# A mixture-of-experts kernel on one core: the last expert prepares nothing for a next one, output tiles are copied and scattered tile by tile, and GpSimd waits once for VectorE

## The chip, the core and the metric

The kernel runs on one core of one Trainium2 chip. The metric is device microseconds (us) of one execution. Before the change it takes 1136.28 us, the median of 3 runs that lie between 1135.86 and 1139.66 us.

## The reference, cut to what matters

```python
# x (4, 512, 512), fside (4, 512, 512), cond (4, 128)
x = x + gated_recurrence(bi_wkv(x, fside, fside, w1, u1, cond))   # W_in, W_decay, W_gate, W_out: 512 x 512
x = x + moe(bi_wkv(x, fside, fside, w2, u2, cond))

def bi_wkv(r, k, v, w, u, cond):        # along t, per channel
    ek, ekv = exp(min(k, 30)), exp(min(k, 30)) * v
    # forward and backward sums a = a * decay + ekv, b = b * decay + ek
    num = fwd(ekv) + bwd(ekv) - ekv + exp(u + k) * v
    den = fwd(ek) + bwd(ek) - ek + exp(u + k)
    return sigmoid(r) * num / max(den, 1e-8) * (0.8 + 0.2 * tf)

def moe(xr):                            # 2048 tokens, 8 experts, top 2, 640 slots for each expert
    probs = softmax(xr @ Wg); gate, expert = top_k(probs, 2)
    h = relu(einsum("ecd,edf->ecf", dispatched, w1))     # w1 (8, 512, 2048)
    out = einsum("ecf,efd->ecd", h, w2)                  # w2 (8, 2048, 512)
    # each token's row is the gate-weighted sum of its two experts' rows
```

## The kernel before, in words

The program has two phases, and in both each engine runs an order of steps that is written out by hand; semaphores tie the engines together.

**The first phase** (`conditioning_and_routing`) works on 4 batches b of 512 tokens, with channels on the partitions. The sums of bi_wkv are made in 16 units u, each a pair of channel tiles of one batch and one of the two bi_wkv calls. For a unit, VectorE runs `backward` and `fold` (scans, L1149 to L1159), `complete` (L1166, L1169) and `ratio` (L1181); ScalarE makes exponentials (`own`, L778 and L782) and the reciprocal of the denominator through Ln and Exp (`first_reciprocal`, L796 and L798); GpSimd makes products of two SBUF tensors: `ek_products` (L356, L357), `products` (L363, L364) and `newton` (L376, L379), adds one term by an accumulating DMA (`own_add`, L370), and sends finished rows to their slots in DRAM (`dispatch`, L389). Two more steps of VectorE matter here. `first_out(b)` (L1194) multiplies `ratios` by the sigmoid `sig`, both in SBUF, and increments `s_r1`. `residual(b)` (L1216) reads the projection in PSUM and writes `xT`; TensorE's `gate(b + 1, k)` (L513) waits for it. `own(u)` on ScalarE waits for `newton(u - 2)`.

The orders that meet around the change are these. GpSimd: `dispatch(0, ...)`, `products(9)`, `ek_products(3, 0)`, `newton(8)`, `own_add(9)`, `products(10)`, `newton(9)`. VectorE: `backward(9)`, `first_out(2)`, `fold(9)`, `complete(9)`, `residual(1)`, `ratio(8)`, `backward(10)`.

**The second phase** (`experts`) runs 8 experts e one after the other. An expert has 640 slots in 5 tiles of 128 (`ST`), and `counts` tells how many hold tokens. The 2048 hidden columns are done in 16 steps of 128. TensorE's `up` makes a hidden step (L1566 to L1568, three products of split float32 parts), ScalarE applies Relu and rounds (L1684, `hh`), VectorE makes the remainder (L1750, `hl`), and TensorE's `down` adds the step into `ps_y` (L1586 to L1588), one PSUM bank for each slot tile, in the order of tiles 2, 3, 4, 0, 1; tiles 2 to 4 are left out where the count does not reach them. ScalarE and VectorE split the next weights in `split` (L1659, L1662; L1711, L1714). An expert with over 512 tokens is "wide": its hidden step is made in two halves.

Every expert also prepares the next one. SyncE loads its rows (`next_rows`), TensorE transposes one tile of them at a time (`turn`, L1536, behind q = 2 to 6 of the 8 rounds q), ScalarE and VectorE copy these into `next_xh` and `next_xl` (L1653, L1705), and at the end copy the whole into `xh` and `xl` (L1688, L1756). The last expert does all this too, though no expert follows.

At the end of an expert ScalarE and VectorE wait until its last `down` is complete (`s_f`), copy the 5 tiles of `ps_y` into `y`, scaled by the gate (L1696: even tiles; L1765: odd tiles), and GpSimd adds each tile's rows to the output in DRAM by an indirect DMA (L1516), tiles 0 to 4 in order. VectorE copies the next gate (L1736) only when all tiles are copied, then reads the count and branches, and only then makes `hl` of the next expert. TensorE meanwhile runs the first two `up` of the next expert.

```python
            for i in range(2, ST):
                with pe.If(count > i * P):
                    slot_tile(i)
            slot_tile(0)
            slot_tile(1).then_inc(s_f, 1)
```

## Time and profile before

| | us |
|---|---|
| median of 3 runs | 1136.28 |
| the profiled execution | 1134.53 |
| its span | 1132.8 |
| PE busy | 1037.4 (92%) |
| DVE busy | 652.9 (58%) |
| ACT busy | 525.7 (46%) |
| POOL busy | 280.2 (25%) |
| share of PE in the chain that ended last | 80% |

The span runs from the first to the last instruction of the program; 1.7 us of the execution lie around it. PE is TensorE's matmul row and PEld its weight loads, DVE is VectorE, ACT ScalarE, POOL GpSimd, SP SyncE; a "q" behind an engine's name is its sequencer. Matmuls are pipelined, so that their durations overlap; what a matmul costs is the distance to the next. "idle before" is the time in which the engine did nothing before an instruction, and the arrow names what released it. The first phase lasts until about 373 us, the experts until the end.

### The profile page before, as it was taken

The numbers are of one execution on the slowest core, as the hardware profiler recorded it, in microseconds if no ns is written. First come the engines' busy times: TensorE is split into PE (matmuls) and PEld (weight loads), VectorE is DVE, ScalarE is ACT, GpSimd is POOL, SyncE is SP. The second block draws the span as 40 slices with busy tenths as digits, with TensorE's granted clock in tenths as the row PEclk, the third lists the DMA queues.
The fourth block names the chain that finished last, engine by engine and source line by source line (L and its number), as shares of the span: only waits on it lengthen the run. The fifth ranks groups of instructions, "written<-read, shape, count | busy, mean of one in ns | idle before, by whom it ended". The sixth has DMA issues, their size and how long they took to land.

```text
span 1132.8 us, 17170 instructions
## 1 busy us (share of the span) xinstructions
PE 1037.4 (92%) x5054; PEld 817.2 (72%) x5055; DVE 652.9 (58%) x948; ACT 525.7 (46%) x844; POOL 280.2 (25%) x233
## 2 busy tenths in 40 slices
PE   3599995899997899999999999999999999999993
PEld 2334542355455799989998999898887888998883
DVE  5899999999983333343334333455564444334552
ACT  5776784676733233343334333445454334334442
POOL 4664746536755100030003000200203002000202
PEclk9999999898988899999999999999999999999997
DMA  6991431223325322262127222744536226222621
GB/s 213 327 303 19 112 78 72 38 93 95 130 47 190 140 74 74 74 166 74 74 74 167 74 74 74 170 145 167 167 111 210 74 74 160 100 91 92 169 74 22
DMA packets 67760, 132.67 MB, mean 117 GB/s; under 512 B 4982, under 2 KB 6042, under 8 KB 67736
## 3 DMA queue, kind: packets, MB, share of 16 engines
q1 hardware_dynamic: 54512, 106.58, 26.7%
q0 software_dynamic: 13008, 25.52, 11.7%
q8 instruction: 12, 0.20, 0.1%
q10 hardware_dynamic: 216, 0.28, 0.1%
q14 instruction: 12, 0.10, 0.0%
HBM read 91.99 MB, written 35.22 MB: 112 GB/s over the span
## 4 chain that ended last, share of the span: by engine, by line
PE 80%; DVE 6%; issue 5%; ACT 3%; DMA 3%; POOL 2%; DVEq 1%; ACTq 0%; SPq 0%; POOLq 0%
PE ps_mm L513 11%; PE ps_y L1586 10%; PE ps_y L1587 10%; PE ps_y L1588 10%; PE ps_h L1566 10%; PE ps_h L1567 10%; PE ps_h L1568 10%; PE ps_mm L530 2%; PE ps_t L1536 2%; PE ps_small L600 1%; DMA rows<-in_x_dram 1%; DVE sums_odd L1159 1%; POOL slots L389 1%; PE ps_x L530 1%; DMA f_rows<-in_fside_BxSxS_dram 1%
## 5 line engine op out<-in xcount | busy, mean ns | idle before, releaser
L1566 PE MATMUL ps_h<-xh,w1h 128*128 128x320 f32 (+4 forms) x768 | 244.8, 319 | 9.9 <-DVE hl L1750 4.4
L1567 PE MATMUL ps_h<-xl,w1h 128*128 128x320 f32 (+4 forms) x768 | 241.0, 314 | 0.0
L1568 PE MATMUL ps_h<-xh,w1l 128*128 128x320 f32 (+4 forms) x768 | 240.8, 313 | 0.0
L1516 POOL DMA_INDIRECT out_dram<-y,token x40 | 64.5, 1613 | 653.8 <-ACT y L1696 590.4
L1750 DVE SCALAR_TENSOR_TENSOR hl<-ps_h,hh 128x320 fp32r<-128x320 f32 (+1 forms) x192 | 106.8, 558 | 189.1 <-ACT hh L1684 183.0
L1586 PE MATMUL ps_y<-w2h,hh 128*128 128x512 f32 x528 | 206.9, 392 | 2.4 <-DVE hl L1750 2.4
L1587 PE MATMUL ps_y<-w2h,hl 128*128 128x512 f32 x528 | 206.3, 391 | 0.0
L1588 PE MATMUL ps_y<-w2l,hh 128*128 128x512 f32 x528 | 206.2, 390 | 0.0
L1714 DVE TENSOR_TENSOR w2l<-raw,w2h 128x512 fp32r<-128x512 f32 x128 | 88.5, 691 | 196.8 <-ACT w2h L1662 196.8
L1684 ACT ACTIVATE hh<-ps_h 128x320 fp32r<-128x320 f32 (+1 forms) x192 | 94.2, 491 | 225.4 <-PE ps_h L1568 225.4
L513 PE MATMUL ps_mm<-ratios,wm 128*128 128x512 f32 x372 | 168.3, 608 | 15.4 <-DVE xT L1216 13.2
L1662 ACT ACTIVATE w2h<-raw 128x512 fp32r x128 | 80.7, 631 | 211.9 <-PE ps_y L1588 211.9
L1566 PEld LDWEIGHTS ps_h<-xh,w1h 128*128 128x128 f32 x768 | 145.1, 189 | 18.1 <-issue 8.0
L1567 PEld LDWEIGHTS ps_h<-xl,w1h 128*128 128x128 f32 x768 | 145.2, 189 | 4.9
L1568 PEld LDWEIGHTS ps_h<-xh,w1l 128*128 128x128 f32 x768 | 145.1, 189 | 2.6
L513 PEld LDWEIGHTS ps_mm<-ratios,wm 128*128 128x128 f32 x372 | 71.2, 196 | 99.0 <-issue 95.4
L1588 PEld LDWEIGHTS ps_y<-w2l,hh 128*128 128x128 f32 x528 | 99.1, 188 | 21.6
L1586 PEld LDWEIGHTS ps_y<-w2h,hh 128*128 128x128 f32 x528 | 99.2, 188 | 20.6 <-issue 3.2
L1587 PEld LDWEIGHTS ps_y<-w2h,hl 128*128 128x128 f32 x528 | 99.2, 188 | 17.1
L1711 DVE TENSOR_TENSOR w1l<-raw,w1h 128x512 fp32r<-128x512 f32 x128 | 88.3, 689 | 16.2 <-ACT w1h L1659 12.1
L1659 ACT ACTIVATE w1h<-raw 128x512 fp32r x128 | 79.8, 623 | 0.0
L1159 DVE TENSOR_TENSOR_SCAN sums_odd<-ps_decay,sums_odd 128x511 f32<-128x511 f32 x32 | 38.3, 1256 | 3.5 <-ACT sums_odd L789 3.5
(206 smaller groups left out, 1179.3 us busy)
## 6 DMA issues: line engine op xcount, KB each, us to landing
raw<-in_L_ffn_w_dram SPq DMA_DIRECT2D x64, 1024.0 KB, 6.9
slots<-r_rows SPq DMA_DIRECT2D x8, 1302.5 KB, 20.2
rows<-slots SPq DMA_DIRECT2D x8, 1302.5 KB, 8.0
rows<-in_x_dram SPq DMA_DIRECT2D x4, 1024.0 KB, 5.3
sums_even<-eukv POOLq DMA_DIRECT2D x8, 512.0 KB, 5.2
sums_odd<-eukv POOLq DMA_DIRECT2D x8, 512.0 KB, 6.0
out_dram<-rows SPq DMA_DIRECT2D x4, 1024.0 KB, 4.7
f_rows<-in_fside_BxSxS_dram SPq DMA_DIRECT2D x3, 1024.0 KB, 5.4
```

Source lines behind the costliest of these rows:

```text
L513: last = nc.tensor.matmul(ps_mm[:, k % 3, :], wm[:, m, dt, e * P:(e + 1) * P], ratio_of(0, b)[:, dt], start=(dt == 0), stop=(dt == CT - 1))
L1566: nc.tensor.matmul(o, w1h[:, j, dt, :], xh[:, dt, lo:hi], start=(dt == 0), stop=False)
L1567: nc.tensor.matmul(o, w1h[:, j, dt, :], xl[:, dt, lo:hi], start=False, stop=False)
L1568: last = nc.tensor.matmul(o, w1l[:, j, dt, :], xh[:, dt, lo:hi], start=False, stop=(dt == CT - 1))
L1586: nc.tensor.matmul(ps_y[:, i, :], hh[:, j, tok], w2h[:, j], start=first, stop=False)
L1587: nc.tensor.matmul(ps_y[:, i, :], hl[:, j, tok], w2h[:, j], start=False, stop=False)
L1588: return nc.tensor.matmul(ps_y[:, i, :], hh[:, j, tok], w2l[:, j], start=False, stop=last)
L1662: a.activation(w2h[:, (j + 1) % 2], raw2[:, bass.ds((c + (j + 1) // FC) % 2, 1), (j + 1) % FC] .rearrange("p o n -> p (o n)"), ACT.Copy).t ...
L1684: a.activation(hh[:, j % 2, lo:hi], ps_h[:, bank, 0:hi - lo], ACT.Relu).then_inc(s_hh, 1 if wide else 2)
L1711: v.tensor_tensor(w1l[:, j % 2], raw1[:, bass.ds((c + j // 2) % 2, 1), :, (j + 2) % FC * P:((j + 2) % FC + 1) * P] .rearrange("p o t q -> ...
L1714: v.tensor_tensor(w2l[:, (j + 1) % 2], raw2[:, bass.ds((c + (j + 1) // FC) % 2, 1), (j + 1) % FC] .rearrange("p o n -> p (o n)"), w2h[:, ( ...
L1750: v.scalar_tensor_tensor(out=hl[:, j % 2, lo:hi], in0=ps_h[:, bank, 0:hi - lo], scalar=0.0, in1=hh[:, j % 2, lo:hi].bitcast(F32), op0=ALU.max,
```

## The change

There are three parts.

1. In the first phase GpSimd waits for `s_r1` to reach 3, which is the end of VectorE's `first_out(2)`, before `newton(8)`.
2. At an expert's end, ScalarE and VectorE no longer wait for the whole last `down`. TensorE increments a semaphore of its own for tiles 2, 3, 4 and 0 as each is finished (at once for a tile that is left out). ScalarE copies tiles 2, 4, 0, VectorE 3, 1, and GpSimd scatters in the order 2, 3, 4, 0, 1. An expert that is not wide still has its tile 4 neither computed nor copied.
3. The last expert loads no rows, turns nothing, copies nothing into `next_xh`, `next_xl`, `xh`, `xl` and the next gate and token, and leaves out the last `split`.

```diff
@@ gpsimd_program, first phase
         ek_products(3, 0)
+
+        pool.wait_ge(s_r1, 2 + 1)
         newton(8)
@@ experts
+    s_out = {i: sem(f"output_tile_{i}_done") for i in (2, 3, 4, 0)}
...
+    EVEN_ORDER, ODD_ORDER = (2, 4, 0), (3, 1)
+    Y_EVEN, Y_ODD = len(EVEN_ORDER), len(ODD_ORDER)
@@ sync_program
         def expert(e, last):
-            next_rows(e)
+            if not last:
+                next_rows(e)
@@ gpsimd_program, second phase
-            for i in range(ST):
+            for i in (*range(2, ST), 0, 1):
                 if i % 2 == 0:
-                    pool.wait_ge(s_ya, Y_EVEN * (e + 1) + i // 2 + 1)
+                    pool.wait_ge(s_ya, Y_EVEN * (e + 1) + EVEN_ORDER.index(i) + 1)
                 else:
-                    pool.wait_ge(s_yv, Y_ODD * (e + 1) + i // 2 + 1)
+                    pool.wait_ge(s_yv, Y_ODD * (e + 1) + ODD_ORDER.index(i) + 1)
@@ down
             for i in range(2, ST):
                 with pe.If(count > i * P):
-                    slot_tile(i)
-            slot_tile(0)
+                    done = slot_tile(i)
+                    if last:
+                        done.then_inc(s_out[i], 1)
+                if last:
+                    with pe.Else():
+                        pe.sem_inc(s_out[i], 1)
+            done = slot_tile(0)
+            if last:
+                done.then_inc(s_out[0], 1)
             slot_tile(1).then_inc(s_f, 1)
@@ tensor_program
                 with pe.Else():
-                    turn_one_of(e, q, 0, ST + 1)
+                    with pe.If(e < NE - 1):
+                        turn_one_of(e, q, 0, ST + 1)
@@ scalar_program (vector_program alike)
                         if j == FC - 1:
                             with act.If(c > NC - 2):
-                                act.wait_ge(s_xh, ST * (e + 2))
-                                a.activation(xh[:], next_xh[:], ACT.Copy).then_inc(s_cur_h, 1)
-                        split(e, c, j)
-                act.wait_ge(s_f, e * FT + (FT + 2))
+                                with act.If(e < NE - 1):
+                                    act.wait_ge(s_xh, ST * (e + 2))
+                                    a.activation(xh[:], next_xh[:], ACT.Copy).then_inc(s_cur_h, 1)
+                                    split(e, c, j)
+                            with act.Else():
+                                split(e, c, j)
+                        else:
+                            split(e, c, j)
...
-                for i in range(0, ST if wide else ST - 1, 2):
-
+                for i in EVEN_ORDER if wide else (2, 0):
+
+                    act.wait_ge(s_out[i], e + 1)
@@ vector_program
-                dve.wait_ge(s_f, e * FT + (FT + 2))
                 dve.wait_ge(s_y0, 1)
                 dve.wait_ge(s_token, e + 1)
-                for i in range(1, ST if wide else ST - 1, 2):
+                for i in ODD_ORDER:
+                    if i == 1:
+                        dve.wait_ge(s_f, e * FT + (FT + 2))
+                    else:
+                        dve.wait_ge(s_out[i], e + 1)
```

GpSimd's order around `newton(8)` before the change, from `products(9)` on (`recip_ready` is `s_rec`):

```order
L363 TENSOR_TENSOR eukv<-euk,kT 128x512 [waits euk_ready]
L364 TENSOR_TENSOR eukv<-euk,kT 128x512
L356 TENSOR_TENSOR ekv<-ek,kT 128x512 [waits ek_ready]
L357 TENSOR_TENSOR ekv<-ek,kT 128x512
L376 TENSOR_TENSOR sums_even<-sums_even,euk 128x512 [waits recip_ready]
L376 TENSOR_TENSOR sums_even<-sums_even,euk 128x512
L379 TENSOR_TENSOR sums_even<-sums_even,euk 128x512 [waits even_own_term_added]
L379 TENSOR_TENSOR sums_even<-sums_even,euk 128x512
```

and with the change:

```order
L363 TENSOR_TENSOR eukv<-euk,kT 128x512 [waits euk_ready]
L364 TENSOR_TENSOR eukv<-euk,kT 128x512
L356 TENSOR_TENSOR ekv<-ek,kT 128x512 [waits ek_ready]
L357 TENSOR_TENSOR ekv<-ek,kT 128x512
L376 TENSOR_TENSOR sums_even<-sums_even,euk 128x512 [waits recip_ready,r1_ready]
L376 TENSOR_TENSOR sums_even<-sums_even,euk 128x512
L379 TENSOR_TENSOR sums_even<-sums_even,euk 128x512 [waits even_own_term_added]
L379 TENSOR_TENSOR sums_even<-sums_even,euk 128x512
```

Nothing has moved; the first `newton` product has a second semaphore to wait for.

ScalarE's order at the end of an expert that is not wide, before, from the last step's `split` to the copies into `y` (`hidden_used` is `s_f`):

```order
L1659 ISA
L1659 ACTIVATE w1h<-raw 128x512
L1661 REGISTER_ALU
L1662 REGISTER_ALU [waits hidden_used]
L1662 ACTIVATE w2h<-raw 128x512
L1673 REGISTER_ALU
L1673 COMPARE_AND_BRANCH
L1690 ISA
L1691 REGISTER_ALU [waits hidden_used]
L1696 ACTIVATE y<-ps_y,gate 128x512 [waits token_ready,y_cleared,gate_ready]
L1696 ACTIVATE y<-ps_y,gate 128x512
```

and with the change (the line numbers are those of the changed file, L1676 and L1679 the split's, L1719 the copy's):

```order
L1705 UNCONDITIONAL_BRANCH
L1676 ISA
L1676 ACTIVATE w1h<-raw 128x512
L1678 REGISTER_ALU
L1679 REGISTER_ALU [waits hidden_used]
L1679 ACTIVATE w2h<-raw 128x512
L1709 UNCONDITIONAL_BRANCH
L1690 REGISTER_ALU
L1690 COMPARE_AND_BRANCH
L1713 REGISTER_ALU
L1719 ACTIVATE y<-ps_y,gate 128x512 [waits token_ready,y_cleared,output_tile_2_done,gate_ready]
L1719 ACTIVATE y<-ps_y,gate 128x512 [waits output_tile_0_done]
```

The wait for the whole `down` ahead of the copies is gone, and each copy waits for its tile. The split now stands in the program twice, once behind the copy of `xh` (ahead of this piece) and once, here, for the rounds that have no such copy.

GpSimd's scatters of the first expert, before:

```order
L1504 COPY token<-next_token 128x5 [waits next_token_ready]
L1508 COPY next_token<-rows 128x5 [waits token_ready,next_rows_in]
L1516 DMA out_dram<-y,token 2048x512 [waits y_cleared,y_even]
L1516 DMA out_dram<-y,token 2048x512 [waits y_odd]
L1516 DMA out_dram<-y,token 2048x512 [waits y_even]
L1516 DMA out_dram<-y,token 2048x512 [waits y_odd]
L1516 DMA out_dram<-y,token 2048x512 [waits y_even]
```

and with the change:

```order
L1511 COPY token<-next_token 128x5 [waits next_token_ready]
L1516 COPY next_token<-rows 128x5 [waits token_ready,next_rows_in]
L1524 DMA out_dram<-y,token 2048x512 [waits y_cleared,y_even]
L1524 DMA out_dram<-y,token 2048x512 [waits y_odd]
L1524 DMA out_dram<-y,token 2048x512 [waits y_even] x2
L1524 DMA out_dram<-y,token 2048x512 [waits y_odd]
```

These are tiles 2, 3, then 4 and 0 from ScalarE, then 1.

## Rows read from the trace of the kernel before

**Rows 1.** Timeline, TensorE: start us, us, instruction, [idle before <- releaser].

```profile
203.00 6.04 PE L513 MATMUL ps_mm<-ratios,wm 128*128 128x512 f32 x8 [13.18 <-DVE xT L1216]
```

**Rows 2.** Timeline, VectorE, 181 to 207 us.

```profile
181.57 11.10 DVE L1194 SCALAR_TENSOR_TENSOR ratios<-ratios,neg_scale,sig 128x2048 f32<-128x2048 f32 x1
...
192.59 4.79 DVE L1159 TENSOR_TENSOR_SCAN sums_odd<-ps_decay,sums_odd 128x511 f32<-128x511 f32 x4
...
198.53 3.67 DVE L1169 TENSOR_SCALAR sums_odd<-sums_odd,den_min 128x512 f32<-128x512 f32 x2
...
204.76 2.05 DVE L1181 SCALAR_TENSOR_TENSOR ratios<-sums_even 128x1024 f32<-128x1024 f32 x1
```

**Rows 3.** Timeline, GpSimd, 180 to 200 us.

```profile
180.70 1.28 POOL L363 TENSOR_TENSOR eukv<-euk,kT 128x512 f32<-128x512 f32 x1
...
184.38 1.26 POOL L357 TENSOR_TENSOR ekv<-ek,kT 128x512 f32<-128x512 f32 x1
185.60 2.47 POOL L376 TENSOR_TENSOR sums_even<-sums_even,euk 128x512 f32<-128x512 f32 x2
188.04 2.48 POOL L379 TENSOR_TENSOR sums_even<-sums_even,euk 128x512 f32<-128x512 f32 x2
...
198.51 1.79 POOL L363 TENSOR_TENSOR eukv<-euk,kT 128x512 f32<-128x512 f32 x1
```

**Rows 4.** Line L1194, all its instructions: duration ns min/median/max.

```profile
L1194 DVE SCALAR_TENSOR_TENSOR ratios<-ratios,neg_scale,sig x4: 1285/2344/11100, 58.9 to 263.8; 128x2048 f32<-128x2048 f32 x3, 128x1024 f32<-128x1024 f32 x1
```

**Rows 5.** Timeline, ScalarE, 188 to 204 us.

```profile
190.61 1.34 ACT L778 ACTIVATE euk<-kT,cap_u 128x512 f32<-128x512 f32 x2 [5.75 <-POOL sums_even L379]
```

**Rows 6.** Waits of VectorE, 205 to 320 us: us in total, times, longest.

```profile
DVE sums_odd L1159 <- ACT sums_odd L789: 1.8, 1, 1.8
DVE xT L1216 <- PE ps_mm L530: 1.1, 1, 1.1
```

**Rows 7.** Busy time by window: PE, PEld, DVE, ACT, POOL, PEclk, DMA share, GB/s.

```profile
203.00:208.00 5.00, 5.00 (x6) 2.16 (x7) 4.89 (x5) 4.94 (x6) 3.55 (x3) 0.52 0.01 3
```

**Rows 8.** Waits of TensorE, 400 to 1120 us.

```profile
PE ps_h L1566 <- DVE hl L1750: 2.6, 3, 0.9
PE ps_y L1586 <- DVE hl L1750: 2.4, 3, 1.2
PE ps_h L1566 <- DVE w1l L1711: 1.7, 2, 0.9
PE ps_h L1566 <- issue: 0.6, 3, 0.3
```

**Rows 9.** Timeline, VectorE, from the first expert to the second.

```profile
491.98 1.41 DVE L1765 TENSOR_SCALAR y<-ps_y,gate 128x512 f32<-128x512 f32 x2 [1.88 <-PE ps_y L1588]
494.10 0.17 DVE L1736 COPY gate<-next_gate 128x5 f32<-128x5 f32 x1 [0.71 <-ACT y L1696]
495.85 0.89 DVE L1750 SCALAR_TENSOR_TENSOR hl<-ps_h,hh 128x320 fp32r<-128x320 f32 x2 [1.58 <-issue]
```

**Rows 10.** The chain that ended last, last expert: start us, us, what.

```profile
1104.39 0.44 PE ps_t L1536 x4
```

**Rows 11.** Timeline, TensorE, the last `down`: end of tile 2, end of tile 1.

```profile
1112.77 0.39 PE L1588 MATMUL ps_y<-w2l,hh 128*128 128x512 f32 x1
...
1114.13 0.39 PE L1588 MATMUL ps_y<-w2l,hh 128*128 128x512 f32 x1
```

**Rows 12.** Timeline, GpSimd, the end: the first and the last of five scatters.

```profile
1116.23 1.57 POOL L1516 DMA_INDIRECT out_dram<-y,token  x1 [53.01 <-ACT y L1696]
...
1123.64 1.54 POOL L1516 DMA_INDIRECT out_dram<-y,token  x1 [0.30 <-issue]
```

**Rows 13.** DMA issues of 1116 to 1119 us (two scatters): us from issue to landing.

```profile
out_dram<-y,token POOLq DMA_INDIRECT x2, 4.9
```

**Rows 14.** DMA issues of 1124 to 1133 us (the last scatter).

```profile
out_dram<-y,token POOLq DMA_INDIRECT x1, 2.7
```

**Rows 15.** DMA queues, 490 to 1133 us: the instruction queue's packets, MB, share.

```profile
q14 instruction: 1, 0.01, 0.0%
```

More of the change, by code:

```diff
@@ L1497, in gpsimd_program, with expert @@
         g.memset(y[:], 0.0).then_inc(s_y0, 1)
-        def expert(e, first):
+        def expert(e, first, last=False):
             pool.wait_ge(s_next_token, e + 1)
@@ L1520, in gpsimd_program @@
         expert(0, True)
-        with pool.Fori(1, NE) as e:
+        with pool.Fori(1, NE - 1) as e:
             expert(e, False)
+        expert(NE - 1, False, True)
         pool.wait_ge(s_add, 16 * ST * NE)
@@ L1678, in body @@
                             with act.If(c > start - 1):
-                                token_high(e, tile_no(c * 2 + more))
+                                with act.If(e < NE - 1):
+                                    token_high(e, tile_no(c * 2 + more))
                         act.wait_ge(s_f, hidden + 1)
@@ L1693, in body @@
                 act.wait_ge(s_token, e + 1)
-                for i in range(0, ST if wide else ST - 1, 2):
+                for i in EVEN_ORDER if wide else (2, 0):
+                    act.wait_ge(s_out[i], e + 1)
                     a.activation(y[:, i], ps_y[:, i, :], ACT.Copy, scale=gate[:, i:i + 1]).then_inc(
-                        s_ya, 2 if i == ST - 3 and not wide else 1)
+                        s_ya, 2 if i == 2 and not wide else 1)
             by_width(act, e, body)
@@ L1745, in body @@
                             with dve.If(c > start - 1):
-                                token_low(e, tile_no(c * 2 + more))
+                                with dve.If(e < NE - 1):
+                                    token_low(e, tile_no(c * 2 + more))
                         for k in range(2 if wide else 1):
@@ L1754, in body @@
                             with dve.If(c > NC - 2):
[L1755 to L1761 removed]
+                                with dve.If(e < NE - 1):
+                                    dve.wait_ge(s_xl, ST * (e + 2))
+                                    v.tensor_copy(xl[:], next_xl[:]).then_inc(s_cur_l, 1)
+                                    dve.wait_ge(s_next, 16 * (e + 1))
+                                    dve.wait_ge(s_gate, e + 1)
+                                    v.tensor_copy(next_gate[:], rows[:, :, bass.ds(e + (C + 1), 1)].rearrange("p i o -> p (i o)")).then_inc(s_next_gate, 1)
+                                    split(e, c, j)
+                            with dve.Else():
+                                split(e, c, j)
+                        else:
+                            split(e, c, j)
                 dve.wait_ge(s_y0, 1)
                 dve.wait_ge(s_token, e + 1)
[L1764 removed]
+                for i in ODD_ORDER:
+                    if i == 1:
+                        dve.wait_ge(s_f, e * FT + (FT + 2))
+                    else:
+                        dve.wait_ge(s_out[i], e + 1)
                     v.tensor_scalar(y[:, i], ps_y[:, i, :], gate[:, i:i + 1], None, ALU.mult).then_inc(s_yv, 1)
```

17 lines of the change are left out of this document (6 added, 11 removed).

## The prediction

> **What bounds the kernel now.** I read the page's chain first. It lies on TensorE for 80% of the span (the table above), so a change pays where TensorE stands still, where it works for nothing, or behind its last matmul. There are three such places. In the first phase it stands still for 13.18 us until 203.00, until VectorE's `residual` writes `xT` [rows 1]. Between experts it waits 2.6 + 2.4 us for VectorE's `hl`, 1.7 us for `w1l`, and 0.6 us for nothing that shows, behind such a wait [rows 8]; inside an expert it never waits. At the end, five scatters follow its last matmul [rows 11, 12].
>
> **Part 1, GpSimd's wait.** VectorE's `first_out(2)` begins at 181.57 and takes 11.10 us [rows 2]; the same line usually takes 2.34 [rows 4]. GpSimd runs eight products of two SBUF tensors without a break from 180.70 to 188.04 + 2.48 = 190.52 [rows 3] (two of `products(9)`, two of `ek_products(3, 0)`, four of `newton(8)`). VectorE's instruction ends at 192.67, 2.15 us behind the last of them: it was held for the whole series, and then ran. With the wait, GpSimd stops behind `ek_products(3, 0)`, at 184.38 + 1.26 = 185.64 [rows 3]. VectorE then ends at 185.64 + 2.2 = 187.8, 4.8 us earlier. Its four scans take 4.7 more, to 192.5. `newton(8)` runs beside them, from 187.9 to 187.9 + 4.9 = 192.8 instead of 190.5, and I take scans as not held: the four of 192.59 take 4.79 [rows 2], 1.2 each, and one of their inputs lies in PSUM.
>
> The next step holds a second gain. `complete(9)`'s two clamps took 3.67 us [rows 2], because `products(10)` began at 198.51 [rows 3], just as they did. `products(10)` waits for ScalarE's `own(10)`, which waits for `newton(8)` [rows 5]. It now begins at 192.9 and needs 2.5 us (four instructions, two of which take 1.34 [rows 5]), so `products(10)` starts at 195.4. Now `complete(9)` lies ahead of it. Its first instruction takes what lies between the scans' end, 192.59 + 4.79 = 197.38, and the clamps at 198.53: 1.2 us. Its clamps took 3.67 while GpSimd's two products ran from 198.5 to 201.3, some 2.8; without those, 0.9 [rows 2, 3]. `complete(9)` waits for the term that GpSimd adds behind `newton(8)`, for which I put 0.2 as its issue. So it ends at 192.8 + 0.2 + 1.2 + 0.9 = 195.1 instead of 198.53 + 3.67 = 202.2. `residual(1)` starts some 7.0 us earlier, and so does TensorE, at 196.0 instead of 203.0.
>
> The Trainium skill ("SBUF — State Buffer", section "Who interferes with whom") says that a VectorE instruction with two SBUF inputs and a GpSimd instruction that reads SBUF exclude each other, and that the one that issues first keeps the shared pair for its whole instruction. Two SBUF inputs is what L1194 has and the scans (one input in PSUM) have not, so kind and place agree. But one instruction's length would end the hold at 181.98, and the row shows eight [rows 2, 3].
>
> Do the 7.0 us last? `newton(8)` is 2.3 us later, but ScalarE's next step behind `own(10)` needs `complete(9)`, so it runs at 195.4 instead of 202.2. VectorE's `ratio(8)` now meets `products(10)` and `newton(9)` at 197.8; it took 2.05 in a like place [rows 2], and if held throughout it would end near 203.9, 3 us before its old end of 206.8 and 4 short of the full shift. VectorE idles 1.8 and 1.1 us for others by 272 us [rows 6] and twice more for 0.7 and 0.5, which takes such a lag up. I see nothing else that is bound to a fixed time. **Term: -7.0**, between -3 (the lag is not taken up) and -9.2.
>
> The lower bound is TensorE's clock. In its first 5 us after the wait the granted clock is 0.52, that is 1.2 GHz [rows 7]; six matmuls end where at 2.4 GHz some 2.2 us would have been saved. After 6 us of idleness it may come back sooner. I take it as unchanged.
>
> **Part 2, tiles one by one, between experts.** VectorE copies the gate at 494.10, behind ScalarE's last `y` copy, and makes `hl` only at 495.85, 1.58 us of its sequencer (the count's load and a branch) behind [rows 9]. Both engines had stood idle until `down` was complete, VectorE 1.88 us, and it then makes two copies in 1.41 us from 491.98 on [rows 9], ScalarE three until 494.0. With the change tiles 2, 3 and 4 are copied under `down`, and only tile 0 (ScalarE, a tile ahead of the end) and tile 1 (VectorE) come near its end. VectorE's is then the last: 491.98 + 0.7 = 492.7 instead of 494.0. So gate and `hl` come 1.3 us earlier, more than any of the waits. I count the two lines that name `hl` and the 0.6 behind them, 5.6 us, less the 0.6 of an expert of under 384 tokens, where VectorE itself comes late from its own `w2l` and the copies gain nothing, less 0.5 for residues: **-4.5**, between -1 (if the 1.58 does not move with the copies) and -5.6. The 1.7 us for `w1l` stay: it waits behind ScalarE's copy of `xh`, which every expert but the last keeps. The tile semaphores are increments on matmuls that are there anyway. One more `If` around `turn` costs TensorE nothing, since its sequencer is ahead inside an expert: no wait there [rows 8].
>
> **Part 3, the last expert.** Five `turn`s go, 0.44 us each on the chain [rows 10]: **-2.2**. Steps without a turn already follow each other without an idle microsecond, so nothing else comes to bound them. The copies into `xh`, `xl` and the last split go too (2.35 us on ScalarE); they lay beside `down` and by themselves give 0, but without them both engines are free when tile 2 is done. The 1.3 MB of rows that are not loaded had no one waiting.
>
> **The end.** Tile 2's last matmul starts at 1112.77, tile 1's at 1114.13 [rows 11], so the first copy and the first scatter come 1.36 us earlier. The five scatters are spaced (1123.64 - 1116.23) / 4 = 1.85 us by GpSimd itself [rows 12], whatever tile they hold, and so the last is issued 1.36 earlier as well. But it is another tile. This expert has at most 320 tokens, so the last scatter was tile 4, without a row, and landed in 2.7 us [rows 14]; now it is tile 1, with 128 rows, and such scatters take 4.9 [rows 13]. The end moves by -1.36 + 4.9 - 2.7 = **+0.8**, between -1.4 (landing as before) and +1.5.
>
> **Sum.** -7.0 - 4.5 - 2.2 + 0.8 = -12.9. Against the profiled execution's 1134.5 this gives 1121.6; the median of the runs lies 1.75 above that execution, so 1136.3 - 12.9 = **1123.4 us**. Runs of this kernel tell a difference from none at about 0.3%, 3.4 us.
>
> **Rivals.**
> - *The hold moves.* `ratio(8)` or a later step is held by a longer series of products, and VectorE's lag reaches TensorE. For it: 11.10 us shows that a series can hold VectorE throughout [rows 2]. Against it: the slack [rows 6]. Part 1 gives -3: 1127.4. Chance 0.15.
> - *The boundary does not shrink.* VectorE's `hl` hangs on something other than the copies. For it: 1.58 us with no releaser [rows 9]. Part 2 gives -0.5: 1127.4. Chance 0.11.
> - *The clock comes back with the shorter wait.* Part 1 gives -9.2: 1121.2. Chance 0.12.
> - *L1194 was not held by GpSimd's series.* By instruction-long exclusion VectorE would have run from 181.98, the 11.10 us have another cause, and the wait gives 0: 1136.3 - 5.9 = 1130.4. This is what the rule of the section cited above would make of it. Against it: 2.15 us from the series' end to the instruction's. Chance 0.03 alone, and 0.03 together with the boundary that does not shrink (1136.3 - 0.5 - 2.2 + 0.8 = 1134.4, no change that can be told).
> - *Slower, by code that no longer stays resident.* ScalarE's and VectorE's loop bodies now hold the split twice, and the other rounds jump over the first copy. In 640 us of experts the instruction queue moves one packet [rows 15], so today all loops are resident. If the jump cost a reload on each of the 32 rounds, at 1.58 us (the longest unexplained gap [rows 9]) that reached TensorE in full, it would lose 32 x 1.58 = 51 us: 1174. It decides from 0.5 us a round, since 32 x 0.5 = 16 is 12.9 + 3.4. Against it: the code grows by about 20 instructions an engine. Chance 0.03.
>
> The Trainium skill ("Runtime: NRT & Kernel Launch", section "Instruction fetch mechanics") says that a taken branch out of a window of two blocks of 256 instructions stalls for a fetch. By that the bodies still fit and this rival falls; no row shows the window.
>
> **Numbers.** The forecast has 0.53, with its own range 1121 to 1126. The range of 8 in 10 takes in the clock and the two rivals at 1127.4 with a margin: 1120 to 1128.5. Faster: 0.53 + 0.15 + 0.11 + 0.12 + 0.03 = 0.94; same 0.03; slower 0.03.
>
> **What would show it.** Right: L1194 near 181.6 takes about 6.3 us and ends near 187.8; the two clamps behind take 0.9; TensorE restarts near 196 and the experts begin 7 us earlier; the waits for `hl` between 400 and 1110 us fall from 5.0 to about 1; the last expert has no L1536; the last scatter starts 8.15 us behind the last matmul's start and not 9.5, and needs about 4.9 to land. Wrong: L1194 still over 10 us, or another VectorE step in the first phase grown by several; TensorE restarting at 196 with the experts less than 5 us earlier; idle TensorE inside experts or packets of the instruction queue there; a last landing much over 5 us.

## The result, and the profile after

The changed kernel takes **1124.97 us**, the median of 6 runs (1121.84 to 1130.62); the kernel before took 1136.07 in 6 runs beside them. The ratio is 0.9891, 95% interval [0.9871, 0.9910]: 11.1 us less in the medians. The forecast was 1123.4, with a range of 1120.0 to 1128.5. In the experiments below the changed kernel was measured again (e4): 1125.34, ratio 0.9900 [0.9876, 0.9924].

Its first profiled execution was the longest of its six. So two executions stand here, that one ("first") and the one of e4 ("second"):

| us | before | after, first | after, second (e4) |
|---|---|---|---|
| the execution | 1134.53 | 1130.62 | 1125.55 |
| span | 1132.8 | 1128.8 | 1123.8 |
| TensorE restarts | 203.00 | 197.08 | 196.53 |
| first `up` of the experts | 374.83 | 373.93 | 369.68 |
| first `up` to the start of the last `down` matmul | 739.30 | 735.03 | 734.29 |
| idle TensorE from 392 us to there | 7.4 | 4.3 | 3.7 |
| from there to the end of the span | 18.67 | 19.87 | 19.79 |

Without the row of idle time, the last three rows are parts of the span and add up to it: in the second execution 5.15 + 5.01 - 1.12 = 9.0 us less than the profiled execution of before. The other 2 us lie in that execution of before: it was 1.5 to 3.1 us below the medians of its kernel (1136.07 to 1137.66 from one set of runs to the next). Below, "lead" is by how much earlier TensorE starts a matmul than in that one execution of before; at 262 us it is the matmul that starts there at 262.50, at 323 us the one at 323.20.

The timeline of TensorE, VectorE and GpSimd in the first execution answers to [rows 1 to 3]:

```profile
197.08 6.23 PE L515 MATMUL ps_mm<-ratios,wm 128*128 128x512 f32 x8 [3.96 <-DVE xT L1218]
...
181.82 7.45 DVE L1196 SCALAR_TENSOR_TENSOR ratios<-ratios,neg_scale,sig 128x2048 f32<-128x2048 f32 x1
189.19 4.79 DVE L1161 TENSOR_TENSOR_SCAN sums_odd<-ps_decay,sums_odd 128x511 f32<-128x511 f32 x4
193.90 1.46 DVE L1168 TENSOR_TENSOR sums_odd<-sums_odd,euk 128x1024 f32<-128x1024 f32 x1
195.40 0.88 DVE L1171 TENSOR_SCALAR sums_odd<-sums_odd,den_min 128x512 f32<-128x512 f32 x2
...
182.15 1.28 POOL L363 TENSOR_TENSOR eukv<-euk,kT 128x512 f32<-128x512 f32 x1
...
185.83 1.27 POOL L357 TENSOR_TENSOR ekv<-ek,kT 128x512 f32<-128x512 f32 x1
189.34 2.49 POOL L376 TENSOR_TENSOR sums_even<-sums_even,euk 128x512 f32<-128x512 f32 x2 [2.24 <-DVE ratios L1196]
191.79 2.49 POOL L379 TENSOR_TENSOR sums_even<-sums_even,euk 128x512 f32<-128x512 f32 x2
194.28 1.31 POOL L370 DMA_DIRECT2D sums_odd<-eukv  x1
```

`first_out(2)` (now L1196) ends at 189.27, 2.17 us behind the end of `ek_products(3, 0)` at 187.10: held for four products and not eight. The two clamps take 0.88 together and not 3.67, and TensorE's wait is 3.96 us long and not 13.18.

Executions differ by some microseconds in when VectorE comes to this instruction (179.58 to 183.32), so the cleanest measure counts from its start to TensorE's restart. That is 21.4 us in all four profiled executions without the wait, and with the wait in this place 14.1 or 15.3: 7.4 us less where GpSimd's first product had begun before VectorE's instruction, 6.2 where VectorE had begun first.

The waits of TensorE from 400 to 1120 us in the second execution answer to [rows 8]:

```profile
PE ps_h L1575 <- issue: 2.7, 4, 1.2
PE ps_y L1595 <- DVE hl L1774: 0.5, 1, 0.5
PE ps_h L1575 <- DVE hl L1774: 0.3, 1, 0.3
```

The waits for `hl` fell from 5.0 to 0.8 us. "issue" rose from 0.6 to 2.7: two of its four stand at the two boundaries where TensorE waited 1.7 us in all for `w1l` before, and are 1.06 and 1.21 us long.

### The profile page after: what moved, and what is told of

It is laid out like the page before. It is cut to its first block, busy times and chain, and to the rows that moved or that the text cites. A ratio compares the mean times of both kernels' runs of the same rounds, so it can differ in the third digit from the quotient of the medians.

```text
span 1128.8 us, 17219 instructions
## 1 busy us (share of the span) xinstructions
PE 1040.3 (92%) x5034; PEld 816.5 (72%) x5035; DVE 644.6 (57%) x939; ACT 519.7 (46%) x836; POOL 279.3 (25%) x232
## 4 chain that ended last, share of the span: by engine, by line
PE 64%; issue 1%; POOL 1%; DVEq 0%; DVE 0%; ACT 0%; POOLq 0%
PE ps_y L1595 11%; PE ps_y L1596 11%; PE ps_y L1597 11%; PE ps_h L1575 10%; PE ps_h L1576 10%; PE ps_h L1577 10%; PE ps_t L1545 1%; POOL out_dram L1524 1%; DVEq L1650 0%; DVE y L1797 0%; DVE hl L1774 0%; ACT y L1719 0%; DVE gate L1759 0%; DVEq L1773 0%; DVEq L1763 0%
## 5 line engine op out<-in xcount | busy, mean ns | idle before, releaser
L1679 ACT ACTIVATE w2h<-raw 128x512 fp32r x127 | 80.1, 631 | 210.2 <-PE ps_y L1597 210.2
L1676 ACT ACTIVATE w1h<-raw 128x512 fp32r x127 | 79.2, 623 | 0.0
```

Of the source, the lines that this page charges most:

```text
L1679: a.activation(w2h[:, (j + 1) % 2], raw2[:, bass.ds((c + (j + 1) // FC) % 2, 1), (j + 1) % FC] .rearrange("p o n -> p (o n)"), ACT.Copy).t ...
```

## The experiments

The kernel before was run beside each set of runs, and every ratio is to it. Each kernel was run 6 times (e2 and e3 12 times), e5 and e8 once.

| run | median us | ratio [95%] | first `up` | up to last `down` | end |
|---|---|---|---|---|---|
| e1 wait only | 1130.10 | 0.9943 [0.9923, 0.9963] | 370.22 | 740.23 | 18.68 |
| e2 tiles only | 1136.05 | 0.9995 [0.9978, 1.0013] | 372.51 | 736.40 | 20.82 |
| e3 last expert only | 1135.25 | 0.9984 [0.9970, 0.9999] | 376.87 | 737.04 | 18.74 |
| e4 changed, again | 1125.34 | 0.9900 [0.9876, 0.9924] | 369.68 | 734.29 | 19.79 |
| e5 tail order | 1117.79 (one) | | 364.69 | 733.98 | 17.33 |
| e6 tail skip | 1121.22 | 0.9859 [0.9831, 0.9887] | 368.31 | 735.76 | 15.78 |
| e7 wait earlier | 1127.45 | 0.9897 [0.9868, 0.9927] | 370.15 | 737.85 | 19.97 |
| e8 pause | 1130.41 (one) | | 374.16 | 734.40 | 19.67 |
| e9 scatters late | 1125.25 | 0.9899 [0.9871, 0.9928] | 369.78 | 733.22 | 20.05 |
| e10 products(15) later | 1125.20 | 0.9892 [0.9861, 0.9923] | 371.27 | 734.87 | 19.69 |
| e11 two waits | 1126.31 | 0.9915 [0.9886, 0.9944] | 370.12 | 734.48 | 19.70 |
| e12 combined | 1117.65 | 0.9832 [0.9808, 0.9855] | 365.85 | 734.38 | 15.76 |

The three last columns are of the profiled execution, as in the table above ("end" is from the start of the last `down` matmul on). A single one of them moves without a cause in the edit: e1, which changes nothing in the experts, has 0.9 us more there than before, and e2, which changes nothing ahead of them, begins them 2.3 us earlier. Over all, the experts begin at 372.5 to 376.9 us in the four executions without GpSimd's wait (mean 374.6) and at 364.7 to 373.9 in the ten with it (mean 369.4).

### e1: the wait alone

```diff
         ek_products(3, 0)
+        pool.wait_ge(s_r1, 2 + 1)
         newton(8)
```

> The kernel before with GpSimd's one wait alone. Theory A (forecast): VectorE's first_out(2) (L1194) ends near 188 to 189, TensorE restarts near 197 instead of 203.0, the experts' first up comes 6 to 7 us earlier (near 368) and the time is 6 to 7 us less, a ratio of 0.9940 to 0.9947. Theory B (read from the profile of the changed kernel, where TensorE led by 7.4 us at 262 us and by only 0.9 us at 374): the lead is given back between 290 and 374 us whatever the execution, because what follows there has its own pace (a clamp of VectorE held by GpSimd, the clock, the loads of rows): the experts start 0 to 2 us earlier and the time is 0 to 2 us less, 0.9980 to 1.0000. Theory C: the loss in that one execution was chance, half of the executions have it: 3 to 4 us less, 0.9965 to 0.9975.

The ratio 0.9943 is 6.5 us less (4.2 to 8.8 by its interval), which is theory A's amount. TensorE restarted at 196.01, 7.0 us earlier, and led by 8.0 us at 262. But the experts began at 370.22, only 4.6 us earlier, which lies between the theories. What was lost lies in VectorE's timeline near 291 us, here of e4, which is alike:

```profile
290.91 3.64 DVE L1171 TENSOR_SCALAR sums_even<-sums_even,den_min 128x512 f32<-128x512 f32 x2
...
291.75 1.28 POOL L363 TENSOR_TENSOR eukv<-euk,kT 128x512 f32<-128x512 f32 x1
292.98 1.28 POOL L364 TENSOR_TENSOR eukv<-euk,kT 128x512 f32<-128x512 f32 x1
```

and of e6, where it did not happen:

```profile
291.01 1.07 DVE L1171 TENSOR_SCALAR sums_even<-sums_even,den_min 128x512 f32<-128x512 f32 x2
...
294.07 1.30 POOL L363 TENSOR_TENSOR eukv<-euk,kT 128x512 f32<-128x512 f32 x1
295.29 1.29 POOL L364 TENSOR_TENSOR eukv<-euk,kT 128x512 f32<-128x512 f32 x1
```

`complete(14)`'s second clamp met `products(15)` and was held for its two products, 2.6 us. In e6 the four DMA instructions of the dispatch ahead of `products(15)` ended later, and it began behind the clamps. With the wait for `s_r1` and `products(15)` in its place, the hold is there in six profiled executions of eight; without that wait in one of four (e3, at 297.8). In the six, TensorE's lead fell by 3.4 us between 262 and 323 us; in e5 and e6 it rose by 0.2. TensorE's own waits put the price a little lower: from 300 to 322 us it waits 3.1 to 3.6 us in the six (1.3 for ScalarE's `z_gate`, the rest for VectorE's) and 1.0 in e5 and e6, so the hold costs it 2.1 to 2.6 us.

Whether the hold comes goes with TensorE's clock some 40 us earlier. Over 244 to 264 us the granted clock (the third number from the end of a row) is 0.91 in all seven of these executions with the hold and 0.83 in all five without it. Here are the windows of before, without the hold, and of e4, with it:

```profile
244.00:264.00 20.00, 18.92 (x84) 12.59 (x83) 18.99 (x37) 13.79 (x17) 6.06 (x5) 0.83 0.13 22
```

```profile
244.00:264.00 20.00, 19.31 (x82) 12.29 (x81) 19.30 (x34) 16.20 (x21) 10.16 (x9) 0.91 0.16 27
```

The two agree in twelve of twelve; that one makes the other was not tested. In e4 `newton(13)` ended 1.3 us earlier than in e6 (286.27 and 287.58) while the clamps began at nearly the same time (290.91 and 291.01), and this brings `products(15)` nearer to them.

### e2: tile by tile alone

```diff
-                act.wait_ge(s_f, e * FT + (FT + 2))
+                    act.wait_ge(s_out[i], e + 1)
...
+            for i in (*range(2, ST), 0, 1):
```

> The kernel before with the tile-by-tile copies and scatters alone; the last expert still prepares a next one. Forecast: TensorE's idle time between 392 us and the last down falls from 7.4 us by 4.5 us at the seven boundaries, the end (last scatter is the full tile 1, lands in 4.9 us and not 2.7) costs 0.8 more: 3.7 us less, ratio 0.9967. Rival: hl comes late for another reason than the copies (count load and branch), idle time stays near 7 us: 0 to +0.8 us, ratio 1.0000 to 1.0007.

The experts took 2.9 us less and TensorE's idle time fell by 3.5, but the end took 2.15 us more and not 0.8: 0.75 us less in the trace, and no difference that the runs could tell. ScalarE's and GpSimd's timeline at the end:

```profile
1105.58 2.35 ACT L1698 ACTIVATE xh<-next_xh 128x2560 fp32r<-128x2560 f32 x1
...
1108.86 1.26 ACT L1706 ACTIVATE y<-ps_y,gate 128x512 f32<-128x512 f32 x2
...
1110.38 1.57 POOL L1519 DMA_INDIRECT out_dram<-y,token  x1 [53.17 <-ACT y L1706]
...
1117.79 1.54 POOL L1519 DMA_INDIRECT out_dram<-y,token  x1 [0.30 <-issue]
```

With the last expert's copy of `xh` and the split still there, tile 2's copy starts at 1108.86, level with the last matmul's start (1108.91). In the changed kernel's first execution it starts 1.10 us before (1107.86 against 1108.96). So the last scatter starts 8.88 us behind that matmul and not 7.91. The end needs parts 2 and 3 together.

### e3: the last expert's omissions alone

```diff
-            next_rows(e)
+            if not last:
+                next_rows(e)
...
+                    with pe.If(e < NE - 1):
+                        turn_one_of(e, q, 0, ST + 1)
```

> The kernel before with the last expert's omissions alone (no rows loaded, nothing turned, copied or split for a next expert); the last expert's copies into y still wait for its whole down. Forecast: five turns of 0.44 us go from TensorE, 2.2 us less, ratio 0.9981, and nothing else moves: the last scatter starts as far behind the last matmul as before (9.5 us) and TensorE's idle time at the boundaries stays near 7.4 us. Rival: the jump over the second copy of the split in every round costs an instruction load or late commands, which would show as more idle TensorE inside the experts: 0 to 10 us more.

As forecast: up to the last `down` 2.26 us less, the end as before (18.74), the waits of TensorE between the experts the same to 0.1 us; the ratio 0.9984 is 1.8 us. That 2.26 meets the forecast 2.2 so closely is partly luck, since e1 shows 0.9 us of difference in the same stretch for nothing. No cost of the second split is to be seen.

### e4: the changed kernel again

> The changed kernel again, for a second profiled execution beside the first, whose 1130.6 us was the longest of six. Theory C: in another execution the lead of TensorE at 262 us (7 us) reaches the experts with at least 4 us left and the profiled time is near 1124. Theory B: the experts' first up is again near 374 and the lead is lost in the same place between 290 and 350 us. By either the median ratio is 0.987 to 0.991.

The lead was 7.9 us at 262 us, 4.5 at 323 and 5.15 at the experts' start. The hold at 291 us is there too, so the fall up to 323 us is not the first execution's own, as theory B has it. What made that execution so long comes later: its lead was 4.1 us at 323 us, but it reached the experts with 0.9. That part is theory C's. The waits of TensorE from 323 to 374 us, the first execution and then e4 (without those of about the same length in both):

```profile
PE ps_t L1621 <- DVE w2l L1400: 4.0, 1, 4.0
...
PE ps_mm L547 <- ACT rows L860: 2.8, 2, 1.4
...
PE ps_small L754 <- DVE dest L1282: 0.7, 1, 0.7
```

```profile
PE ps_t L1621 <- DVE w2l L1400: 3.1, 1, 3.1
...
PE ps_small L754 <- DVE dest L1282: 1.6, 1, 1.6
PE ps_mm L547 <- ACT rows L860: 0.3, 1, 0.3
```

From 323 us on the first execution falls 3.8 us behind e4. The waits for ScalarE's rows and for `w2l` are 3.4 us longer in it and the one for `dest` 0.9 shorter, 2.4 in all; why ScalarE and VectorE came late there was not followed further.

### e5 and e6: the last expert's scatters

e5 changes their order, e6 leaves out the empty ones:

```diff
-            for i in (*range(2, ST), 0, 1):
+            for i in (2, 0, 1, 3, 4) if last else (*range(2, ST), 0, 1):
```

```diff
+            if last:
+                count = pool.value_load(counts[0:1, NE - 1:NE], min_val=1, max_val=CAP)
...
+                if last and i > 1:
+                    with pool.If(count > i * P):
+                        scatter(i, s_part[i])
```

> The changed kernel, but the last expert's five scatters go in the order of tiles 2, 0, 1, 3, 4, so that the last one has no row. If the landing of the last scatter is what gave back most of the earlier start, the last scatter again starts about 7.9 us behind the last matmul's start (all copies are done 3 us before), lands in 2.7 us and not 5.2, and the end comes 17.3 us behind the last matmul's start and not 19.8. If the queue works tiles one after the other, so that the empty ones wait behind the full ones, it lands later than 2.7 us and the end gains less than 1 us.

> The changed kernel, but in the last expert GpSimd reads the count and leaves out the scatters of tiles that hold no token (3 and 4 here). Two scatters fewer at 1.85 us each: the last one starts 7.9 - 3.7 = 4.2 us behind the last matmul's start, lands in about 5.2, and the end is 3.7 us earlier than with all five, 16.1 us behind the last matmul. Against the kernel before: ratio 0.9870 to 0.9880 where the changed kernel has 0.9891 to 0.9900. Rival: the branches and waits on GpSimd, or the copy of tile 1, set the pace instead: less than 2 us.

The last scatter of e5, in GpSimd's timeline and in the DMA issues (us to landing at the end of the row):

```profile
1106.57 1.54 POOL L1524 DMA_INDIRECT out_dram<-y,token  x1 [0.31 <-issue]
```

```profile
out_dram<-y,token POOLq DMA_INDIRECT x1, 2.7
```

and of e6, whose last scatter is the third:

```profile
1108.28 1.54 POOL L1508 DMA_INDIRECT out_dram<-y,token  x1 [0.30 <-issue]
```

```profile
out_dram<-y,token POOLq DMA_INDIRECT x1, 5.3
```

Last `down` matmuls started at 1098.67 and 1104.07, so the last scatters start 7.90 and 4.21 us behind them, and the ends are 17.33 and 15.78: both as expected (17.3, 16.1). In the changed kernel GpSimd's sequencer leaves its wait for the last landing 5.25 us behind that scatter's start; before it was 2.74. The full tile at the end costs 2.5 us. (e5's single time also has the earliest first phase of all: its `first_out(2)` starts at 179.58, 2.0 us before that of the profiled execution of before, which its edit does not explain.)

### e7: the wait two products earlier

```diff
         products(9)
+        pool.wait_ge(s_r1, 2 + 1)
         ek_products(3, 0)
-        pool.wait_ge(s_r1, 2 + 1)
         newton(8)
```

> The changed kernel with GpSimd's wait two instructions earlier, ahead of ek_products(3, 0) instead of behind it, so that the series beside L1196 (first_out(2)) is two products and not four. If VectorE is held until the series ends, L1196 ends 2.2 us behind the end of products(9), near 185.8, and takes about 2.5 us less than with the wait in its place (4.0 to 4.9 against 6.2 to 7.4); its scans then end near 190.6. ek_products and newton(8) then run as one series of six from 186 to 193.5, and complete(9)'s clamps are held to its end, so TensorE restarts at 196 to 197, as in the changed kernel: ratio like the changed kernel's, 0.988 to 0.991. If VectorE were held for one instruction only and its length came from something else, L1196 would keep its 6 to 7 us.

VectorE's and GpSimd's timeline:

```profile
182.19 5.01 DVE L1195 SCALAR_TENSOR_TENSOR ratios<-ratios,neg_scale,sig 128x2048 f32<-128x2048 f32 x1
...
193.34 2.77 DVE L1170 TENSOR_SCALAR sums_odd<-sums_odd,den_min 128x512 f32<-128x512 f32 x2
...
183.75 1.29 POOL L364 TENSOR_TENSOR eukv<-euk,kT 128x512 f32<-128x512 f32 x1
187.28 1.26 POOL L356 TENSOR_TENSOR ekv<-ek,kT 128x512 f32<-128x512 f32 x1 [2.24 <-DVE ratios L1195]
...
192.18 3.65 POOL L379 TENSOR_TENSOR sums_even<-sums_even,euk 128x512 f32<-128x512 f32 x2
```

The hold follows the length of the series: 11.10 us beside eight products, 7.4 or 6.2 beside four, 5.0 or 3.8 beside two (e11). The larger of each pair is where VectorE began first, by 0.33 to 0.34 us, the smaller where GpSimd's first product was 0.9 us old. In all fourteen profiled executions the instruction ends 2.15 to 2.17 us behind the end of the series, here 187.20 - 185.04 = 2.16. The other half of the expectation is wrong in its mechanism: the clamps were not held to the end of `newton(8)` but took turns with its last two products (1.37 and 1.48 against 2.25 and 1.44), and TensorE restarted at 196.91, as with the wait in its place.

### e8: a pause instead of the wait

```diff
-        pool.wait_ge(s_r1, 2 + 1)
+        for _ in range(8):
+            pool.nop(nofuse=True)
         newton(8)
```

> The changed kernel with eight empty instructions of GpSimd in the place of its wait: a short pause (0.3 to 0.6 us) in the series without a tie to VectorE. If the hold is one of back-to-back issue, VectorE gets in during the pause, L1196 ends 2.2 us behind ek_products(3, 0) as with the wait (6.2 to 7.4 us long), and newton(8) starts up to 2 us late, behind it. If VectorE does not get in, L1196 is held through newton(8) again and takes 9 to 11 us as in the kernel before, and TensorE restarts near 202.

```profile
180.58 11.10 DVE L1196 SCALAR_TENSOR_TENSOR ratios<-ratios,neg_scale,sig 128x2048 f32<-128x2048 f32 x1
...
183.39 1.27 POOL L357 TENSOR_TENSOR ekv<-ek,kT 128x512 f32<-128x512 f32 x1
184.61 2.49 POOL L376 TENSOR_TENSOR sums_even<-sums_even,euk 128x512 f32<-128x512 f32 x2
...
202.01 2.90 PE L515 MATMUL ps_mm<-ratios,wm 128*128 128x512 f32 x3 [13.18 <-DVE xT L1218]
```

The empty instructions made no pause at all (183.39 + 1.27 = 184.66, and the next product starts at 184.61), and with the series whole the hold is whole: 11.10 us, TensorE idle for 13.18 as before. So it is the break in the series that frees VectorE, and not a few more instructions in GpSimd's stream. Whether a short real pause would do stays open.

### e9: scatters behind all copies

```diff
+            if not last:
+                pool.wait_ge(s_yv, Y_ODD * (e + 1) + Y_ODD)
             for i in (*range(2, ST), 0, 1):
```

> The changed kernel, but in the first seven experts GpSimd starts its first scatter only when all tiles are copied; the copies stay tile by tile. In the changed kernel VectorE's load of the next count takes 0.63 to 0.97 us at the four wide boundaries where two tiles' scatters are already under way, against 0.31 to 0.33 at all boundaries before. If the scatters are what slows the load, it takes 0.31 to 0.35 again at all seven, hl comes 0.3 to 0.6 us earlier there and TensorE's idle time from 392 us to the last down falls from 3.7 to 4.3 us to 2.6 to 3.2 us: 1.0 to 1.5 us less than the changed kernel. If it is the load's place behind VectorE's own copies, it stays at 0.6 to 1.0 and the idle time at 3.6 to 4.3 us.

VectorE's load of the next count, the seven after the first, as ns min/median/max, before, in e4 and in e9:

```profile
L1633 DVEq TENSOR_LOAD <-counts x7: 306/317/327, 494.4 to 1051.8; - x7
```

```profile
L1650 DVEq TENSOR_LOAD <-counts x7: 306/633/968, 488.1 to 1043.0; - x7
```

```profile
L1652 DVEq TENSOR_LOAD <-counts x7: 309/314/327, 488.6 to 1042.6; - x7
```

Idle time fell to 2.9 us and TensorE no longer waits for `hl` at all. In e4 the load is slow (0.63 to 0.97) at the four wide boundaries, where it follows the start of the first scatter by more than 2 us (488.14 to 485.89 at the first), and not at the other three, where it follows by 1.2 to 1.3; before it followed by 0.2 to 0.75. The experts took 1.1 us less than in e4; the median does not show it, since it is less than the interval.

### e10 and e11: two other places in the first phase

```diff
         dispatch(1, 0, 2)
-        products(15)
         dispatch(1, 2, 4)
+        products(15)
```

> The changed kernel with GpSimd's products(15) behind dispatch(1, 2, 4) instead of ahead of it. In four of six profiled executions with the wait, VectorE's clamp of complete(14) (L1171 near 291 us) took 3.23 us beside products(15), in two 0.67, and in the kernel before 0.67. If this hold is what takes part of the lead away, the clamp takes 0.5 to 0.7 us, TensorE's lead over the kernel before at 314 to 348 us is the same as at 262 us (7 us) and not 2.5 us less, the experts start 2 to 3 us earlier than in e4, and the median falls by 1 to 2 us (in a third of the executions there was no hold to lose). If the lead is lost there for another reason (the clock's half level from 314 to 325 us, the loads of rows), the experts start no earlier than 368 us.

```profile
292.12 1.07 DVE L1171 TENSOR_SCALAR sums_even<-sums_even,den_min 128x512 f32<-128x512 f32 x2
...
298.84 4.88 DVE L1224 SCALAR_TENSOR_TENSOR sig<-ratios,neg_scale,sig 128x2048 f32<-128x2048 f32 x1
...
299.03 1.29 POOL L363 TENSOR_TENSOR eukv<-euk,kT 128x512 f32<-128x512 f32 x1
```

The clamp was free and `second_out(2)` held in its place, 4.88 us against 2.32: the hold had moved, and with it the loss (a lead of 6.7 us at 262 us, 3.3 at 323). The time is the changed kernel's, where 1 to 2 us less had been expected.

e11 has e7's edit and one wait more:

```diff
         ek_products(3, 0)
+        pool.wait_ge(s_den, 9 + 1)
         newton(8)
```

> The changed kernel with GpSimd's wait ahead of ek_products(3, 0), as in e7, and a second one ahead of newton(8), for VectorE's complete(9) (s_den at 10). In e7 complete(9) ran beside newton(8): 1.47 us and two clamps of 1.37 and 1.48, 4.3 us in all instead of 2.3. Clear of it, complete(9) ends 2 us earlier, near 194, and TensorE restarts near 194.5 instead of 196.9. But newton(8) starts behind it, near 194 instead of 189.7, so own(10), ratio(8) and newton(9) come 2 to 4 us later. If VectorE's slack takes that up, as it took up the lag in the changed kernel, the time is 1 to 2 us less than the changed kernel's; if not, TensorE waits again by 262 us and the time is the same or 1 to 3 us more.

TensorE restarted at 193.41, practically without a wait, and stood still 11 us later:

```profile
193.41 3.67 PE L515 MATMUL ps_mm<-ratios,wm 128*128 128x512 f32 x8 [0.20 <-DVE xT L1218]
...
208.66 4.11 PE L515 MATMUL ps_mm<-ratios,wm 128*128 128x512 f32 x5 [4.28 <-ACT z_in L817]
```

Its lead at 262 us was 7.4 us, that of the changed kernel (7.4 and 7.9). The restart gained 3.1 us over e4's, and the clock more: behind a wait of only 0.20 us the granted clock stayed at 1.00 (193.4 to 203.4 us), and the eight matmuls took 3.67 us where e4's took 6.34 at 0.50. The next wait, 4.28 us, and the half level behind it (0.66 over 209 to 214 us) took all of this: that wait is for ScalarE, which makes `z_in` behind `own(10)` in its order, and `own(10)` waits for `newton(8)`, now 4 us later.

### e12: what the runs point to, together

e6's skipped scatters, e9's wait, and `products(15)` behind both dispatches with a wait of its own:

```diff
         dispatch(1, 2, 4)
         own_add(14)
+        pool.wait_ge(s_r2, 2 + 1)
+        products(15)
         own_add(15)
```

> The changed kernel with what the runs point to: e6's empty scatters left out in the last expert (about 3.9 us at the end), e9's scatters behind all copies in the other experts (the count's load back to 0.31 to 0.33, TensorE's idle time from 392 us on 2.8 to 3.1), and products(15) behind both dispatches with a wait for VectorE's second_out(2) (s_r2 at 3). In e10, without that wait, the hold moved from the clamp to second_out(2) (L1224, 4.88 us). If it is the overlap with GpSimd's series that costs there, the clamp near 291 us takes 0.5 to 0.7, L1224 2.3 to 2.4, the scans behind them keep their 1.2 each beside products(15), and TensorE's lead at 323 us is 1 to 2.5 us above that of e4: ratio to the kernel before 0.983 to 0.985. If the hold moves once more (the scans L1161 or L1201 behind), VectorE comes no earlier to products_y(3) and only the two others stay: 0.985 to 0.986.

```profile
288.50 1.07 DVE L1172 TENSOR_SCALAR sums_even<-sums_even,den_min 128x512 f32<-128x512 f32 x2
...
295.21 2.33 DVE L1225 SCALAR_TENSOR_TENSOR sig<-ratios,neg_scale,sig 128x2048 f32<-128x2048 f32 x1
297.46 4.79 DVE L1162 TENSOR_TENSOR_SCAN sums_odd<-ps_decay,sums_odd 128x511 f32<-128x511 f32 x4
...
297.63 1.28 POOL L363 TENSOR_TENSOR eukv<-euk,kT 128x512 f32<-128x512 f32 x1 [0.89 <-DVE sig L1225]
```

The kernel takes **1117.65 us**, 0.9832 of the kernel before, and its six runs lie within 3 us (1116.56 to 1119.42) where the changed kernel's lie within 8 to 9 (and e1's within 4.4). Nothing is held near 290 us; `products(15)` lies beside scans with one input in PSUM, which keep their 1.2 us each. TensorE's lead was 10.3 us at 262 us and 9.5 at 323, a fall of 0.8 and not 3.4. Its height owes something to chance: `first_out(2)` starts at 180.11 here, 1.5 us before that of before. The interval of the ratio (0.9808 to 0.9855) also reaches into what was expected without the gain near 290 us (0.985 to 0.986), so for that part the trace speaks and the times do not.

## Why the prediction was right, point by point

- **The sum** was -12.9 and the medians say -11.1 (e4's ratio says 0.0100 x 1137.45 = 11.4). It was 1.5 to 1.8 us too large by these, which is within the noise: the interval of the first ratio runs from 10.2 to 14.7 us. The terms that missed in the traces all missed the same way, so the forecast did not come right by errors that cancel.
- **Part 1, -7.0.** e1 gives -6.5 (0.0057 x 1137.45; the interval is 4.2 to 8.8), and the starts of the experts give 374.6 - 369.4 = 5.2 in the mean of the profiled executions. L1194 was to take 6.3 us and took 6.24 where GpSimd had begun first (e1), 7.45 where it had not; the forecast had no term for that second case, which costs 1.2 us. TensorE was to restart at 196.0 and did at 196.01 in e1; from the start of L1194 that is 14.07 us where the forecast had 14.4, and 15.26 in the first execution, so the agreement to 0.01 is luck. That VectorE is held for the whole series and ends 2.2 us behind it held in every execution; the rival that it was not held has fallen. One step was wrong: "`complete(9)` waits for the term that GpSimd adds behind `newton(8)`". It waits for ScalarE and its own scans only, and starts as these end, at 193.90, ahead of the `own_add(9)` at 194.28. The 0.5 us that this would have given went into GpSimd's series, which ended 0.4 us later in e1, and into `complete(9)`'s first instruction, which took 1.48 us beside `newton(8)` and not 1.2. (The two products beside the old clamps ended at 199.73 + 1.78 = 201.5, not 201.3; nothing hangs on it.)
- **"I see nothing else that is bound to a fixed time"** did not hold. The rival *the hold moves* is partly true: `ratio(8)` was not slowed (1.77 us, 2.05 before), but `complete(14)` met `products(15)` near 291 us and cost TensorE 2.1 to 2.6 us in six executions of eight. It is not made by the wait alone, since e3 has it without one; the forecast had no term for it. One of its own signs of being wrong, "TensorE restarting at 196 with the experts less than 5 us earlier", came in the first execution (0.9 us) and in e1 (4.6), and "the experts begin 7 us earlier" in none of the changed kernel's two.
- **Part 2, -4.5.** TensorE's idle time fell by 3.1 and 3.7 us (e2: 3.5). Of the six waits for `hl` [rows 8] two are left in e4, 0.25 and 0.50 us. The term was about 1 us too large for two reasons: the 1.58 us of VectorE's sequencer was taken to move along unchanged, but its count load grew from 0.32 us to between 0.63 and 0.97 beside the earlier scatters (e9); and the two boundaries behind `w1l` were to keep 1.7 us and have 2.3, with no releaser in the profile. It is part 2 that makes these 0.6 us, since e2 has them and e3 has not, but `w1l` is not their cause: at the first of the two TensorE started 0.62 us behind the end of `w1l` before (788.56 to 789.18) and 1.11 behind it in e4 (781.03 to 782.14). What it waited for stays open.
- **Part 3, -2.2.** e3: 2.26 us in the trace, 1.8 (0.1 to 3.4) in the runs.
- **The end, +0.8.** It is +1.2 and +1.1. The last scatter starts 7.91 us behind the last matmul (8.15 forecast, 9.51 before), but lands in 5.25 and not 4.9, and 0.3 us more lies behind the landing. e5 shows that the landing is the cause, e2 that the earlier start needs part 3.
- **The clock.** The window of e4 behind the restart:

```profile
197.00:202.00 5.00, 5.00 (x7) 1.90 (x7) 4.89 (x6) 4.94 (x6) 5.00 (x4) 0.51 0.31 54
```

  The granted clock is 0.51 over these 5 us, as it was 0.52 [rows 7]. Over the 5 us behind the restart it is 0.50 in six of the eight executions with the wait in this place, 0.66 in e5 and 0.70 in e6; without the wait it is 0.50 to 0.53 in three and 0.68 in e2. So it does not come back sooner for the shorter wait, and that rival has fallen.
- **Code.** The rival on the slower side has fallen: no more idle time inside experts in e3.
- The Trainium skill's rule ("SBUF — State Buffer", section "Who interferes with whom") names the right pair of engines and the right kind of instruction; what it makes of a scan with one input in PSUM (no conflict) is what e6 and e12 show beside `products(15)`, 1.2 to 1.3 us each. That the loser waits for one instruction is not what L1194 shows: it was held for eight, four or two. The clamps and `newton` in e7 do take turns by the instruction. What decides between the two stays open.

## What to carry to other kernels

Where a VectorE instruction takes several times its usual length, look for a row of GpSimd products without a gap beside it: what matters is the length of that row, and one wait that breaks it, or its move beside VectorE instructions that read PSUM, takes the hold away. Follow a lead through the trace to the end: here a third of it was taken again 90 us later by the same kind of meeting, and in the one trace with a second wait it was kept. At a program's end, put the smallest transfers last or leave the empty ones out, since the landing of the last one is in the time in full.

## What the runs showed of the hardware that was not expected

- VectorE is held by GpSimd's series even where it began 0.33 us before it (7.44 us beside four products in e4).
- Eight empty GpSimd instructions between two products leave no gap between them (e8).
- At the boundaries between experts a load of one number by VectorE's sequencer takes 0.31 to 0.33 us, and 0.63 (e4) to 1.17 (e8) where the first scatter started over 2 us before; ScalarE's, a little earlier, keeps 0.27 to 0.30.
- In the last expert a scatter whose rows are all left out lands in 2.7 us when it comes last (3.6 to 3.9 for the empty one right behind the three with rows), and tile 1's of 128 rows in 5.1 to 5.5 when it comes last; GpSimd starts the next one 1.85 us later in either case.
- Behind a wait of TensorE of 2.7 to 13.2 us the granted clock was 0.50 to 0.70 over the next 5 us; behind one of 0.20 us it stayed at 1.00 (e11).
